# Record stage of a graph network: mask in PSUM, 16-partition loads of the features, tile row on 64 partitions

## What is computed

```python
edge_index = jnp.stack([src, dst])
x = _layernorm(x + _L0_gnn_ref(x, edge_index, ...))                  # 4 layers: segment_sum(x[src], dst), two linears, batch norms
x = _layernorm(x + _L1_gnn_ref(x, edge_index, edge_attr_64, ...))    # messages x[col] @ W_T + edge_attr_64 @ T_w, summed by row
x = _layernorm(x + _L2_gnn_ref(x, edge_attr_16, ...))                # ea = silu(edge_attr_16 @ We + be); 4 layers of relu(x[src] + ea)
x = _layernorm(x + _L3_gnn_ref(x, edge_attr_128, ...))               # attention, Eh = edge_attr_128 @ WE
```

## Time and profile before

| | us |
|---|---|
| median of 3 runs | 11243.84 |
| lowest and highest | 11237.96, 11248.44 |
| profiled execution: its own time | 11201.28 |
| profiled execution: span | 11199.5 |

### The profile page before, as it was taken

How to read it: one execution, slowest core, us unless ns; L and a number is a source line. 1 busy time by engine, 2 the same in 40 slices (tenths; PEclk the granted TensorE clock), 3 DMA queues, 4 the chain that set the end, 5 groups by cost and what they waited for, 6 DMA issues and landing times.

```text
span 11199.5 us, 235901 instructions
## 1 busy us (share of the span) xinstructions
PE 7585.0 (68%) x62128; PEld 6593.0 (59%) x62129; DVE 7054.8 (63%) x17000; ACT 3599.6 (32%) x7576; POOL 4802.8 (43%) x4705
## 2 busy tenths in 40 slices
PE   4789990377776877773799777777777765454554
PEld 3466660376665766763677766766667654444443
DVE  5566670355756656556665688787787885555554
ACT  0122220220602504204501634535436443333333
POOL 0667776335053161350044063161360545666663
PEclk7555555798998998996999998999999986666665
DMA  8666665995674864850797696896896964454556
GB/s 329 183 190 193 193 193 33 129 293 157 227 250 122 316 193 162 296 161 12 211 379 319 253 321 231 304 331 225 313 322 227 322 218 131 128 132 128 133 131 80
DMA packets 1747195, 2371.76 MB, mean 212 GB/s; under 512 B 516388, under 2 KB 1046151, under 8 KB 1746651
## 3 DMA queue, kind: packets, MB, share of 16 engines
q1 hardware_dynamic: 1292446, 1275.33, 36.8%
q0 software_dynamic: 318912, 1049.17, 29.4%
q10 hardware_dynamic: 135677, 45.42, 1.7%
HBM read 1485.10 MB, written 955.49 MB: 218 GB/s over the span
## 4 chain that ended last, share of the span: by engine, by line
PE 22%; issue 10%; another core or an unknown queue 8%; DVE 5%; ACT 4%; SPq 2%; DMA 1%; DVEq 1%; ACTq 1%; POOL 0%; POOLq 0%
PE ps L837 8%; PE ps L859 7%; PE ps L856 4%; SPq L623 2%; PE ps L877 1%; ACT onehot L1120 1%; DVE gath L1517 1%; ACT gath L1110 1%; ACT gath L1089 1%; PE ps L869 1%; ACT big L1242 0%; DMA big<-rec 0%; DMA big<-kv_table,src_at 0%; DVE stats L1747 0%
## 5 line engine op out<-in xcount | busy, mean ns | idle before, releaser
L739 POOL DMA_INDIRECT gath<-msg_units,unit_at_d x2176 | 2160.0, 993 | 3821.0 <-DMA msg_units<-gath 2611.9
L859 PE MATMUL ps<-onehot,gath 128*128 128x125 f32 x17408 | 2498.7, 299 | 975.1 <-issue 421.9
L859 PEld LDWEIGHTS ps<-onehot,gath 128*128 128x128 f32 x17408 | 2249.5, 207 | 1224.2 <-issue 965.5
L837 PE MATMUL ps<-big,onehot 125*128 x29376 | 1919.5, 223 | 712.8 <-DVE onehot L1478 462.8
L837 PEld LDWEIGHTS ps<-big,onehot 125*128 125x128 bf16 x29376 | 1805.9, 97 | 829.1 <-issue 786.1
L1089 ACT ACTIVATE gath<-ps 128x512 f32<-128x512 f32 x2448 | 1426.6, 598 | 1208.8 <-PE ps L837 1016.6
L1510 DVE TENSOR_TENSOR onehot<-ps,node_d 128x500 f32<-128x500 f32 x2176 | 1464.3, 673 | 187.5 <-issue 180.6
L1478 DVE TENSOR_SCALAR onehot<-row_b,part 125x512 bf16<-125x512 uint8 x2448 | 1136.6, 482 | 688.9 <-PE ps L837 685.8
L749 POOL DMA_INDIRECT big<-kv_table,src_at x1088 | 1111.5, 1022 | 837.4 <-DVE gath L1605 367.9
L711 POOL DMA_INDIRECT rec<-big,idx_ring x832 | 963.4, 1158 | 418.6 <-issue 353.7
L1529 DVE TENSOR_TENSOR big<-big,ps 128x125 f32 x2176 | 610.0, 280 | 764.3 <-PE ps L859 696.1
(11 more groups left out here) (219 smaller groups left out, 8702.8 us busy)
## 6 DMA issues: line engine op xcount, KB each, us to landing
msg_units<-gath SPq DMA_DIRECT2D x2176, 256.0 KB, 2.2
big<-ea_units SPq DMA_DIRECT2D x1088, 256.0 KB
ea_units<-rec SPq DMA_DIRECT2D x16, 4352.0 KB
rec<-gath SPq DMA_DIRECT2D x272, 256.0 KB, 6.2
big<-rec SPq DMA_DIRECT2D x272, 256.0 KB
big<-in_attr_t SPq DMA_DIRECT2D x208, 256.0 KB
rec<-big SPq DMA_DIRECT2D x1, 43296.0 KB, 152.4
gath<-msg_units,unit_at_d POOLq DMA_INDIRECT x2176
```

Of the source, the lines that this page charges most:

```text
L739: pool.indirect_dma_start(att_slot(q) if way == "attr" else gath[:, q, :], None, units, bass.IndirectOffsetOnAxis(ap=unit_at[w][:, g:g + 1 ...
L837: ins = pe.matmul(ps[:, r, c], hots_t[0:NT, r, c], upper[0:NT, ds(at_[q] + b, D)], start=b == NA * NODES_PAD, stop=b == LOW)
L859: ins = pe.matmul(ps[:, RING + r, 0:NT], unit_ring[:, q, j, :], hots[:, r, j, :], start=j == 0, stop=j == UNIT - 1)
```

## The change

Three things change in the record stage. The mask `earlier` is copied once into bank 1 of PSUM, and L1410 reads it there. The four blocks of 16-value features lie in partitions 0 to 63 without their rows of ones between them; one row of ones stands at partition 64, written once by DVE, and the bias row of the weights lies there too, so the loads are of 16 partitions and the matmul's contraction has 65 rows. The row of tile numbers is broadcast to 64 partitions, of which DVE reads 51.

```diff
-A16_4 = 4 * (A16 + 1)
+A16_4 = 4 * A16 + 1
...
         lower = earlier[:, (PER - 1) * P:]
+        earlier_ps = ps[:, 1, :]
...
-        tile_b = part_of_big([BKT, RING, PER * P // 4]).bitcast(U8)
+        tile_b = part_of_big([64, RING, PER * P // 4]).bitcast(U8)
...
                 for k in range(PER):
-                    sp.dma_start(a16_w[k * (A16 + 1):(k + 1) * (A16 + 1), k, :], A["ea_w"]).then_inc(loaded, 16)
+                    sp.dma_start(a16_w[k * A16:(k + 1) * A16, k, :], A["ea_w"][0:A16, :]).then_inc(loaded, 16)
+                    sp.dma_start(a16_w[PER * A16:A16_4, k, :], A["ea_w"][A16:A16 + 1, :]).then_inc(loaded, 16)
...
-                        sp.dma_start(tile_b[:, q, :], dst_tile_row[cols].partition_broadcast(BKT)).then_inc(tile_in[q], 16)
+                        sp.dma_start(tile_b[:, q, :], dst_tile_row[cols].partition_broadcast(64)).then_inc(tile_in[q], 16)
...
                         for k in range(PER):
-                            sp.dma_start(a16_t[k * (A16 + 1):(k + 1) * (A16 + 1), q, :],
-                                         A["attr16_t"][:, ds(((i * RING + q) * PER + k) * P, P)]).then_inc(att_in[q], 16)
+                            sp.dma_start(a16_t[k * A16:(k + 1) * A16, q, :],
+                                         A["attr16_t"][0:A16, ds(((i * RING + q) * PER + k) * P, P)]).then_inc(att_in[q], 16)
...
             def scatter(n):
-                dve.wait_ge(loaded, 16 * (5 + PER))
+                dve.wait_ge(keys_kept, -(-COLS // P))
+                ch.link(dve.tensor_copy(earlier_ps, earlier))
+                dve.wait_ge(keys_out[0], 32 * 4)
+                dve.wait_ge(keys_out[1], 32 * 3)
+                dve.wait_ge(vals_in, 16)
+                ch.link(dve.memset(a16_t[PER * A16:A16_4, :, :], 1.0))
+                dve.wait_ge(loaded, 16 * (5 + 2 * PER))
...
-                    dve.tensor_scalar(turned_e[:, q % 2, :], tile_b[:, q, :], part[0:BKT, 0:1], None, ALU.is_equal)\
+                    dve.tensor_scalar(turned_e[:, q % 2, :], tile_b[0:BKT, q, :], part[0:BKT, 0:1], None, ALU.is_equal)\
...
-                                                            bucket[:, ds(g * PER + k, 1)], earlier[:, (PER - 1 - k) * P:],
+                                                            bucket[:, ds(g * PER + k, 1)], earlier_ps[:, (PER - 1 - k) * P:],
```

More of the change, by code:

```diff
@@ L585, in scatter @@
                 sp.wait_ge(zeroed, 16 * 2)
-                sp.wait_ge(loaded, 16 * (5 + PER))
+                sp.wait_ge(loaded, 16 * (5 + 2 * PER))
                 for q in range(RING):
@@ L819, in lap @@
                           .then_inc(rec_mm, 1)
-                pe.wait_ge(loaded, 16 * (5 + PER))
+                pe.wait_ge(loaded, 16 * (5 + 2 * PER))
                 laps(pe, LOADS, lap)
```

## The result

The changed kernel takes 11,370.78 us (median of 4 runs, 11,364.8 to 11,379.82), the kernel before 11,244.3 in the same session: ratio 1.0108, 95% interval 1.0096 to 1.0120. It is slower by 126 us. The forecast was 11,164, faster by 80.

The account below looks back on a forecast made before the run. Candidates were POOL and PE; with scatters freed, PE would bound the record stage at 5.99 us per group against 6.50. Three quarters of 107 us, 80, took the profiled 11,201.3 to 11,121; with 42.6 for the median, 11,164, range 11,125 to 11,290.

Parts of the forecast that it names:

- the cause of the holds: Record stage: a DVE instruction with two SBUF operands holds a POOL scatter starting under it; visible cause of 161 us.
- the rival that it doesn't matter: Mask in PSUM: scatters stay held through the key operand in SBUF, only the loads gain, 25 to 45 us; chance 0.06.
- the 0.67 us per group that the text weighed: DVE's rank operations: if two SBUF sources run at half throughput, PSUM saves DVE 0.67 us per group; time unchanged.
- PE's wait for the table copy: Record stage: PE's wait for ACT's table copy, 122.0 us in 50 waits, would fall to some 30.
- With POOL's need at 5.15 us, PE is the bound with 5.99: Record stage, per group: POOL's need falls from 5.83 us, PE sets the pace; without stalls the stage wins 107 us.
- three quarters, 80 us: Record stage: the part of the full 107 us taken as gain, a cadence of 6.12 us per group.
- SP can run ahead: Feature loads: if spread over more DMA engines, the single engine is relieved and SP gets ahead with issuing.
- the late signals get worse: Record stage: unbroken scatters delay PE's signals, 6.83 us per group, 68 us slower, 11,312; chance 0.22.
- a gain of 0 to 30: New partition counts of the loads: worth 0 to perhaps 30 us alone, through SP and the late signals.
- groups 33 to 36: Record stage before the change: twelve scatters in a row, then a 4.80 us stop; 6.83 us per group.
- L581's issues short and even: SP's feature loads: a sign that would show the loads are spread over DMA engines.
- The stage's start: Four more one-row DMAs and DVE's setup before the first scatter: cost 0, or 12 us without the 94 us cover.

Follow-up runs that it names:

- a pause: On the fast chip, a POOL memset of 128x768 after each group's four scatters: 1.0076 added to the kernel before, 0.9966 added to the mask alone.
- holds added: Mask alone plus one unused 128x512 DVE operation per group with two SBUF operands, which can hold scatters: 11,160.35 us, ratio 1.0048 to the kernel before.
- the pair above: Mask alone plus one unused 128x512 DVE operation per group, its mask operand in PSUM (ratio 1.0081) or in SBUF (1.0048).
- one long pause: Mask alone plus a POOL memset of 128x768 after each group's four scatters, on a chip with late signals: 11,158.02 us, ratio 1.0047 to the kernel before.
- the kernel with the operation in PSUM: Mask alone plus one unused 128x512 DVE operation per group that reads the mask in PSUM: 11,199.22 us, ratio 1.0081 to the kernel before.
- the table's trend: Kernels with more or less of the mask in PSUM, added operations or a pause: scatter means 0.981, 1.027, 1.084, 0.976, 1.158 us; ratios 1.0081, 1.0070, 1.0048, 1.0047, 1.
- the one with one load: The changed kernel with a group's four feature loads as one DMA of 64 partitions: 11,203.8 us, ratio 1.0074 to the kernel before.
- the kernel before with the pause and with the added operation: The kernel before plus a POOL memset of 128x768 per group: 1.0001; or plus an unused 128x512 DVE operation with two SBUF operands: 1.0038.

## Why the prediction was wrong

*What held.* PE's clock (0.52 of full speed before in 370 to 1700 us, 0.50 now); the cause of the holds; L713's mean near 0.98 us (977 ns) and none at 1.97 (longest 1306 ns), so the mask's place does free POOL, and the rival that it doesn't matter falls. DVE pays nothing for PSUM: 734 ns for 512 columns against 741, 331 against 336 for 128; nor did it gain the 0.67 us per group that the text weighed. PE's wait for the table copy is gone from the list, as forecast.

*The step that failed* is the sum's "With POOL's need at 5.15 us, PE is the bound with 5.99" and the "three quarters, 80 us" taken from it, with its ground that a POOL with 0.84 us to spare per group would catch up after a stall. In it SP's own time stands at nothing ("SP can run ahead"). PE's lost time did not vanish; it became another wait. In the stretch from 370 to 1700 us PE was busy 1187 us before and in the changed kernel it is busy 1106, waiting for the loads that SP issues late, while POOL idles for ACT's copy. SP is the engine that ran out of slack: its waits went from 167 us to 0.7. The stage was bound neither by PE nor by POOL; the likeliest account is a circle in which ACT gets its signal late and POOL stops behind it, while SP, slowed, brings the loads late. That each link causes the next is argued, not shown. The 122.0 us that PE waited were a symptom, not the size of the gain. The 116 us of the chip without late signals don't rescue the sum, though they are near its 107: there a pause had made POOL the bound of the kernel before, and POOL's cadence fell from 6.32 to 5.79 us, not PE's wait.

The same stretch of the changed kernel, columns as in the earlier trace rows:

```profile
370.00:1700.00 1330.00, 1106.16 (x4048) 778.97 (x4048) 829.63 (x2759) 255.74 (x740) 724.41 (x741) 0.50 0.57 175
```

*The rival "the late signals get worse"* had the sign and the picture right: POOL runs ahead in an unbroken row and stops. Its mechanism is not borne out as it stands, since ACT's signals came no later than before (710.1 us of waits against 705.8, and 757.4 against 744.5 with holds added); what changed is how long POOL, PE and DVE wait. Its test was met: the gaps of 4 to 5 us came, though in one group of four (52 of 208) and not of three. Its price was too low: 6.83 us per group and +68 us, against 7.11 and +126. The missing part has two terms. The loads are 16 us alone and 36 on top of the mask, where the text gave them a gain of 0 to 30 because "nobody waits for these loads in steady state"; now PE waits 195.5 us for them and DVE 328.7 for the tile row. (The text had two prices for the loads, 0 to 30 us here and 25 to 45 in the rival on the mask's place; both had the wrong sign.) And the mask alone costs 80 to 107 us, not 68, perhaps because the pattern of groups 33 to 36 was taken from a kernel whose holds still broke up the rest; no run tests that. The argument against the rival ("a stretch with a stall has fewer holds anyway", so the pattern may be the stall's result) was wrong as a ground for doubt: the pair above shows that holds shorten POOL's stops for ACT (69.5 us against 241.0).

*"L581's issues short and even"* failed: the median went up (230 to 317 ns for the features, 264 to 511 for the tile row) and single groups take 7 us (long issues are not new: the longest single one was 6.4 us before and is 5.3 now). A load of 16 or 64 partitions costs SP more issue time than one of 17 or 51, and this was not in the sum.

*The stage's start* was rightly costed at zero: the first scatter starts at 348.5, before it was 351.3.

**What stays open.** Shown is that moving the mask makes most of the loss, and that added holds or one long pause give back 43 and 45% of it (39 and 41 of 91 us, counting from the kernel with the operation in PSUM; for the pause that is the nearest control on its chip). That the rest comes from the released scatters too is only argued, by the table's trend, and a part that the reads of PSUM cause is not excluded for it. That SP's lost slack is the path fits every run but the one with one load, and no run frees SP by itself. Why a signal of PE comes late, and why SP's steps are slow while POOL scatters, is not known. No kernel was found that beats the kernel before on a chip with late signals: 0.9992 for the 16-partition loads alone is no difference.

## What to carry to other kernels

Busy time that you free on an engine is worth something only if that engine, or the one it blocks, sets the pace; where several engines idle in turn behind late signals, first ask what the freed engine does with its time. If it is an issuer of indirect DMAs, running faster can make the others wait longer. Look at the waits of the queue that only issues loads, too: here it was the one whose slack had gone, and it stood in no sum. When you find a row in the trace of before that shows the bad pattern in small (here twelve scatters in a row and a gap), price the case in which it becomes the rule at more than that row shows, and give it a chance like the forecast's. And count the issue time of every DMA whose partition count you change.

## What the runs showed of the hardware

- The same kernel took 10,295.56 us on one chip and 11,105 to 11,244 in the five other sessions. On that chip the mask in PSUM, with a pause in both kernels, wins 1.1% (0.9966 against 1.0076); on two of the others the mask, without a pause in either kernel, costs 0.7 and 0.9%. The records of SP differ as well: counting the steps between neighbouring SP records of 370 to 1690 us that last 0.62 to 0.80 us, there are 786 in the kernel before, 828 with the mask alone, and 11 to 19 in the kernels of the fast chip (296 and 610 in the kernel before with the pause and with the added operation).
- An operation of DVE with two SBUF operands holds a running scatter of POOL until about 0.85 us after its own end (of 169 scatters over 1.1 us beside the added operation, 159 end 0.83 to 0.85 us after it); with one operand in PSUM it doesn't (longest scatter 1.37 us), and costs DVE the same (735 and 731 ns).
- SP's issue of a load depends on its partitions, and not in their order: 230 ns at 17, 317 at 16, 264 at 51, 511 at 64 (medians).
